# A convolution and Fourier kernel: channels c and c+16 share a Fourier block, and two intermediate layouts are turned round

## The chip, the cores and the metric

The kernel runs on one core of one Trainium2 chip. The metric is the device time of one execution in microseconds (us), the median over several runs. The program is written engine by engine: TensorE (PE; its weight loads are PEld), VectorE (DVE), ScalarE (ACT), GpSimd (POOL) and SyncE (SP, which issues transfers). Each engine runs its own list in order and waits on semaphores.

## The reference, cut to what matters

The input x is (8, 32, 64, 64): 8 images, 32 channels, 64 rows, 64 columns, all float32. A prologue (a per-pixel adaptive 3x3 filter) makes a new x. Then four layers follow, each of which is

```python
z = conv3x3(x, Kj); z = batchnorm(z); z = relu(z); z = conv3x3T(z, Kj)
x = batchnorm(x + 0.1 * z)
# per channel, with a real table t (channel x 64 x 64):
x = real(ifft2(fft2(x) * t))
```

The last line is the Fourier part. It is a sum over columns (W), a sum over rows (H), a multiplication by the table, and the way back over H and then W. The change touches the data between these sums.

## The kernel before, in words

Images are taken in four pairs (bp = 0 to 3), and each pair in four quarters (q = 0 to 3), so there are 16 steps of each kind in a layer and 64 in the four layers. A convolution step is 12 matmuls of 128x32 weights on 128x512 of data; each float32 matmul is two matmul instructions and two weight loads, so it shows as x24 in the trace. The four column tiles of a convolution (32 columns of the array each) run side by side.

The Fourier part of a quarter goes through these steps, each into one PSUM bank of 128x512, emptied by the engine named:

- `turn` (L958): four transposes put the image columns and the two images of a pair on the partitions; ACT empties them into `turned` (`keep_turned`, L491), 64 times one instruction of 128x512. Before, `turned` holds for each channel its 64 rows side by side, "(c h)": neighbouring channels of one row, which is how the bank is read, are 64 elements (256 bytes) apart.
- `fwdW` (L969): four matmuls; the stationary operand, which the weight load brings in, is the data (128 neighbouring elements of `turned`, two channels of 64 rows), and the moving operand is the constant C_FW. DVE empties the bank with four copies of 64x256 (`keep_fwdW`, L765) into `freqw`. The first quarter of a pair waits for all four `turn` quarters of it.
- `slot0`, `fwdH`, `slot0c` (L978, L985, L993): here the data moves and a constant is stationary. `slot0` waits for all four `fwdW` quarters of the pair. It moves 64 columns that stand 32 elements (128 bytes) apart; `slot0c` moves 64 columns that are neighbours. DVE multiplies by the table into `spec` (L772, L783).
- `invH` (L1003): four matmuls whose stationary operand is the data in `spec` (neighbouring elements) and whose moving operand is C_IH. The bank is emptied by four instructions of 64x256 into `backw` (`back_from_h`): by ACT (L504), or for the quarters q = 1 and 3 of pairs 2 and 3 by DVE (L789). `backw` is one of two buffers, which the profile names work (even pairs) and spare (odd pairs). Before, it holds for each image row h the 32 channels, "(h c e)": the rows of one channel, which is how the bank is read, are 32 elements (128 bytes) apart.
- `invW` (L1014): four matmuls with 128 neighbouring elements of `backw` as the stationary operand (4 image rows of 32 channels) and C_IW moving. ACT empties it into x with the batchnorm's scale (L517).

The order of steps on PE is written out by hand in `layer_steps` and is the same for all engines: the first Fourier pairs stand between the steps of the second convolution (L840 with Z), pairs 2 and 3 in a stretch without convolutions, and the last `invH` and `invW` steps between the first steps of the next layer's first convolution (L840 with X). Eight banks are handed out in that order, and a step waits until its bank's former use has been emptied.

Of the kernel before, what the change touches and what calls it, by code (L numbers as in the profile page):

```python
# [6 lines left out]
B, C, H, W = 8, 32, 64, 64  # L7
R = 128 // C
G = H // R
# [16 lines left out]
CH = 4  # L26
# [9 lines left out]
C_ID, C_FW, C_FH, C_IH, C_IW, C_HH, C_HC, C_AVG, C_ERE, C_EIM = (128 * i for i in range(10))  # L36
# [9 lines left out]
P_L = P_GB + 2  # L46
P_L9 = P_L + C * 3
P_ALL = P_L9 + C * TAPS
# [96 lines left out]
def build(nc, x_in, par, w1, b1, w2, b2, cst, sel, idb, out):  # L145
# [3 lines left out]
    with ExitStack() as ctx:  # L149
# [11 lines left out]
        turned, freqw, spec, rest, backw0 = work  # L161
# [15 lines left out]
        backw = (backw0, spare[:, 0:WORK])  # L177
# [4 lines left out]
        def cm(c, n=128, k=128):  # L182
            return cstS[0:k, c:c + n]
# [15 lines left out]
        def bank(n):  # L199
            return psum[:, n % BANKS, :]  # L200
# [78 lines left out]

        def back_from_h(n, bp, q):  # L280

            src = bank(n).rearrange("p (c t h) -> p t c h", c=4, t=2)
            dst = backw[bp % 2][:, :].rearrange("p (h c e) -> p e c h", c=C // 2, e=2)[:, :, 4 * q:4 * q + 4]
            return [(dst[64 * part:64 * part + 64, e], src[64 * e:64 * e + 64, part]) for e in range(2) for part in range(2)]

        def in_dram(t, image, r):
# [111 lines left out]
        def _(act):  # L398
# [88 lines left out]
            def keep_turned(j, c):  # L487
                n, q = NUMBER["turn", j, c], c % Q
                bk.full(n)
                dst = turned[:, :].rearrange("p (c h) -> p h c", h=H)[:, 16 * q:16 * q + 16, :]  # L490
                nc.scalar.activation(dst, bank(n).rearrange("p (h c) -> p h c", c=C),  # L491
                                     ACT.Identity).then_inc(drained[n % BANKS], 1)

            def keep_slot0(j, bp):
# [5 lines left out]
            def keep_invH(j, c):  # L500
                n = NUMBER["invH", j, c]
                bk.full(n)
                for dst, src in back_from_h(n, c // Q, c % Q):
                    last = nc.scalar.activation(dst, src, ACT.Identity)  # L504
                last.then_inc(drained[n % BANKS], 1)
# [14 lines left out]
            for j in range(DEPTH):  # L520
                for what, *at in layer_steps(j):
                    if (what, at) == ("var", [j, 1]):
                        root(j, 1)
                        act.wait_ge(bn_ready, 2 * j + 1)
                        relu_pair(j, 0)
                        for i in range(4):
                            square(j, i)
                        relu_pair(j, 1)
                        relu_pair(j, 2)
                        act.wait_ge(table_done, j + 1)  # L530
                    elif (what, at) == ("var", [j, 2]):
                        root(j, 2)
                    elif what == "turn":
                        keep_turned(*at)
                        if at == [j, Q - 1]:
                            relu_pair(j, 3)
                    elif what == "slot0c":
                        keep_slot0(*at)
                    elif what == "invH" and not turned_by_dve(at[1] // Q, at[1] % Q):
                        keep_invH(*at)  # L540
                    elif what == "invW":
                        keep_invW(*at)
                    elif what == "conv1":
                        keep_conv1(*at)
# [5 lines left out]
        def _(dve):  # L550
# [234 lines left out]
            def keep_invH(j, c):  # L785
                n = NUMBER["invH", j, c]
                bk.full(n)
                for dst, src in back_from_h(n, c // Q, c % Q):
                    last = nc.vector.tensor_copy(dst, src)  # L789
                last.then_inc(drained[n % BANKS], 1)  # L790
# [36 lines left out]
        def _(pe):  # L827
# [134 lines left out]
            def forward_w(j, c):  # L962
                n, (bp, q) = NUMBER["fwdW", j, c], divmod(c, Q)
                bk.claim(n)
                for i in range(Q if q == 0 else 0):
                    bk.result(NUMBER["turn", j, bp * Q + i])
                for i in range(4):
                    p = (4 * q + i) * 128
                    last = nc.tensor.matmul(bank(n)[:, 128 * i:128 * i + 128], turned[:, p:p + 128],  # L969
                                            cm(C_FW), start=True, stop=True)  # L970
                last.then_inc(filled[n % BANKS], 1)

# [34 lines left out]
            def inverse_w(j, c):  # L1007
                n, (bp, q) = NUMBER["invW", j, c], divmod(c, Q)
                bk.claim(n)
                for i in range(Q if q == 0 else 0):  # L1010
                    bk.result(NUMBER["invH", j, bp * Q + i])
                for g in range(CH):
                    p = (CH * q + g) * 128
                    last = nc.tensor.matmul(bank(n)[:, 128 * g:128 * g + 128], backw[bp % 2][:, p:p + 128], cm(C_IW),  # L1014
                                            start=True, stop=True)
                last.then_inc(filled[n % BANKS], 1)

            for j in range(DEPTH):
                for what, *at in layer_steps(j):
                    if what == "table":  # L1020
                        table(*at)
                    elif what == "mean":
                        average(what, *at, mean_in, 0)
                    elif what == "var":
                        average(what, *at, var_in, 4)
                    elif what == "conv1":
                        conv1(*at)
                    elif what == "conv2":
                        conv2(*at)
                    elif what == "turn":  # L1030
                        turn(*at)
                    elif what == "fwdW":
                        forward_w(*at)
                    elif what == "fwdH":
                        forward_h(*at)
                    elif what == "slot0":
                        slot_0(*at)
                    elif what == "slot0c":
                        slot_0_back(*at)
                    elif what == "invH":  # L1040
                        inverse_h(*at)
                    elif what == "invW":
                        inverse_w(*at)


def constants():

    n = np.arange(64)
    th = 2 * np.pi / 64
    k = np.arange(SL)  # L1050
    cos, sin = np.cos(th * np.outer(n, k)) / 8, np.sin(th * np.outer(n, k)) / 8
    alternating = np.cos(np.pi * n) / 8
    c = np.zeros((128, C_ALL), np.float64)
    c[:, C_ID:C_ID + 128] = np.eye(128)

    fw = np.stack([cos, -sin], 1)
    fw[:, 1, 0] = alternating
    c[:, C_FW:C_FW + 128] = np.einsum("wts,bd->wbdts", fw, np.eye(2)).reshape(128, 128)

    iw = np.stack([2 * cos, -2 * sin], 1)  # L1060
    iw[:, 0, 0], iw[:, 1, 0] = 1 / 8, alternating
    c[:, C_IW:C_IW + 128] = np.einsum("wts,bd->tbswd", iw, np.eye(2)).reshape(128, 128)


    cos, sin = np.cos(th * np.outer(n, n)) / 8, np.sin(th * np.outer(n, n)) / 8
    complex_h = np.block([[cos, -sin], [sin, cos]])
    hartley_h = np.kron(np.eye(2), cos + sin)
    c[:, C_FH:C_FH + 128] = complex_h
    c[:, C_IH:C_IH + 128] = complex_h.T
    c[:, C_HH:C_HH + 128] = hartley_h  # L1070
    c[:, C_HC:C_HC + 128] = np.round(hartley_h @ complex_h, 6)
    c[:, C_AVG:C_AVG + 128] = np.kron(np.ones((R, R)), np.eye(C)) / R
    for part in range(2):
        freq = np.where(k > 0, k, 32 * part)
        for i in range(3):
            q = part * 6 + i * 2
            a = th * n * (i - 1)
            s = slice(64 * part, 64 * part + 64)
            c[q, C_ERE:C_ERE + 128][s], c[q + 1, C_ERE:C_ERE + 128][s] = np.cos(a), -np.sin(a)
            c[q, C_EIM:C_EIM + 128][s], c[q + 1, C_EIM:C_EIM + 128][s] = np.sin(a), np.cos(a)  # L1080
            c[q, C_CS:C_CS + SL], c[q + 1, C_CS:C_CS + SL] = np.cos(th * freq), np.sin(th * freq)
            c[q, C_ONE] = 1
            c[q, C_SGN], c[q + 1, C_SGN] = 1, -1
    for form in range(2):
        c[C * form:C * (form + 3), C_MASK + form] = -1.0 / TAPS
    sel = np.zeros((3, R, TAPS, TAPS, R, C), np.float32)
    for r in range(R):
        for k in range(TAPS):
            sel[:, r, k, k, r, :] = 1
    return c.astype(np.float32), sel.reshape(3 * R * TAPS, TAPS * 128), np.eye(128, dtype=np.float32)  # L1090
# [55 lines left out]
```

## Time and profile before

| what | value |
|---|---|
| median of 3 runs | 877.1 us (876.7 to 879.67) |
| profiled execution | 876.81 us, span 875.0 us |
| mean granted TensorE clock | 0.945 of full speed |
| PE busy | 800.4 us (91%), 5704 matmul instructions |
| PEld busy | 397.6 us (45%) |
| DVE busy | 533.4 us (61%) |
| ACT busy | 396.6 us (45%) |
| prologue, up to the first Fourier step | about 240 us |
| one layer | about 173 us (the first `turn` of layers 0 and 1 starts at 240.07 and 413.61) |

A row of the trace of the form "L969 PE MATMUL psum<-cstS,work" names the line, the engine, the operation, the output and the inputs. For matmuls the moving operand stands first and the stationary one second, so "cstS,work" has the data as its stationary operand, and "work,cstS" has the data moving. "PEld LDWEIGHTS" is the load of the stationary operand; it overlaps with the matmuls before it.

### The profile page before, as it was taken

Reading aid. Unit: us, or ns where it says so; the run is one execution under the profiler, and the core shown is the slowest. Engines: PE = TensorE matmul, PEld = TensorE weight load, DVE = VectorE, ACT = ScalarE, POOL = GpSimd, SP = SyncE. Lnnn points to the kernel's source line nnn. Section 1 sums busy time; section 2 is a strip of 40 time slices with the busy share of each in tenths; the row PEclk is TensorE's granted clock in tenths of the full one; section 3 lists DMA queues with packets and bytes.
Section 4 is the critical chain, followed back from the end, with each engine's and each line's share of the span. In section 5 each row is a group of like instructions: output and inputs, shape, how many; then the busy total and the mean of one; then the engine's idle time right before and its main releaser. Section 6 shows DMA issues by size and latency. Waiting matters only on the chain.

```text
span 875.0 us, 14085 instructions
## 1 busy us (share of the span) xinstructions
PE 800.4 (91%) x5704; PEld 397.6 (45%) x5704; DVE 533.4 (61%) x982; ACT 396.6 (45%) x579; POOL 121.6 (14%) x108
## 2 busy tenths in 40 slices
PE   4698999998999799999997999899979999999793
PEld 1133333332245584432455854234568532345683
DVE  1499888964676565336765743286648332866571
ACT  1121122211855655328466643384575534736654
POOL 0277777760000000000000000000000000000000
PEclk9699899999899989998999999999989998999997
DMA  9999120209200022670000227600003274000035
GB/s 178 184 166 143 29 50 1 50 1 207 70 1 1 1 50 49 140 156 32 1 1 1 50 50 167 159 1 1 1 1 68 46 176 103 1 1 1 1 86 108
DMA packets 74570, 55.44 MB, mean 63 GB/s; under 512 B 69661, under 2 KB 69662, under 8 KB 70410
## 3 DMA queue, kind: packets, MB, share of 16 engines
q1 hardware_dynamic: 69130, 53.25, 31.6%
q10 hardware_dynamic: 5376, 1.30, 1.0%
q8 instruction: 46, 0.75, 0.4%
q14 instruction: 18, 0.15, 0.1%
HBM read 16.25 MB, written 4.19 MB: 23 GB/s over the span
## 4 chain that ended last, share of the span: by engine, by line
PE 72%; DVE 17%; SPq 3%; issue 2%; ACT 2%; DMA 1%; POOL 1%; DVEq 0%; POOLq 0%
PE psum L840 37%; DVE work L765 9%; PE psum L985 6%; PE psum L1003 5%; PE psum L1014 5%; PE psum L958 4%; PE psum L903 4%; PE psum L913 3%; SPq L296 3%; PE psum L969 2%; DVE work L789 2%; PE psum L865 2%; ACT Z L479 1%; DVE work L689 1%; POOL work L392 1%
## 5 line engine op out<-in xcount | busy, mean ns | idle before, releaser
L840 PE MATMUL psum<-Z,wts 128*32 128x512 f32 x1536 | 183.2, 621 | 2.8 <-ACT Z L479 2.5
L840 PE MATMUL psum<-X,wts 128*32 128x512 f32 x1536 | 175.2, 595 | 2.7 <-DMA X<-X 2.7
L765 DVE COPY work<-psum 64x256 f32<-64x256 f32 x256 | 107.9, 421 | 34.0 <-PE psum L969 30.3
L662 DVE BATCH_NORM_STATS2 stats<-Z 128x6 f32<-128x512 f32 x64 | 44.3, 693 | 113.1 <-ACT Z L430 113.0
L392 POOL TENSOR_TENSOR work<-work 128x512 f32<-128x512 f32 x76 | 98.9, 1301 | 74.6 <-DVE work L689 70.7
L491 ACT ACTIVATE work<-psum 128x512 f32<-128x512 f32 x64 | 63.8, 1101 | 75.2 <-PE psum L958 74.8
L430 ACT ACTIVATE Z<-psum 128x512 f32<-128x512 f32 x64 | 38.2, 596 | 129.4 <-PE psum L840 129.4
L840 PEld LDWEIGHTS psum<-Z,wts 128*32 128x32 f32 x1536 | 45.6, 113 | 112.4 <-issue 101.7
L479 ACT ACTIVATE Z<-Z,small 128x512 f32<-128x512 f32 (+1 forms) x96 | 87.6, 964 | 5.2 <-DVE small L741 4.7
L840 PEld LDWEIGHTS psum<-X,wts 128*32 128x32 f32 x1536 | 44.5, 109 | 98.7 <-issue 92.7
L756 DVE SCALAR_TENSOR_TENSOR X<-psum,X 128x512 f32<-128x512 f32 x64 | 43.8, 685 | 58.2 <-PE psum L840 56.6
L504 ACT ACTIVATE work<-psum 64x256 f32<-64x256 f32 x96 | 58.9, 614 | 30.9 <-PE psum L1003 29.8
L1003 PEld LDWEIGHTS psum<-cstS,work 128*128 128x128 f32 x512 | 58.9, 192 | 15.7 <-issue 15.7
L504 ACT ACTIVATE spare<-psum 64x256 f32<-64x256 f32 x96 | 58.6, 611 | 14.0 <-PE psum L1003 12.9
L1003 PE MATMUL psum<-cstS,work 128*128 128x128 f32 x512 | 62.8, 279 | 0.5 <-ACT work L497 0.5
L969 PE MATMUL psum<-cstS,work 128*128 128x128 f32 x512 | 63.0, 278 | 0.0
L985 PE MATMUL psum<-work,cstS 128*128 128x496 f32 x128 | 61.6, 610 | 1.3 <-DVE work L789 1.3
L969 PEld LDWEIGHTS psum<-cstS,work 128*128 128x128 f32 x512 | 59.4, 192 | 6.7 <-issue 6.7
L913 PE MATMUL psum<-work,selS 108*128 108x512 bf16 x144 | 52.6, 416 | 2.9 <-ACT work L406 1.3
L689 DVE TENSOR_TENSOR work<-Z,psum 128x512 f32<-128x512 f32 x68 | 44.4, 673 | 9.2 <-PE psum L913 8.8
L783 DVE TENSOR_TENSOR work<-psum,tabT 128x496 f32<-128x496 f32 x64 | 40.6, 666 | 11.7 <-PE psum L985 11.4
L759 DVE BATCH_NORM_STATS2 stats<-X 128x6 f32<-128x512 f32 x64 | 44.4, 694 | 2.2
(96 smaller groups left out, 796.7 us busy)
## 6 DMA issues: line engine op xcount, KB each, us to landing
X<-X SPq DMA_DIRECT2D x32, 520.0 KB, 5.4
Z<-Z SPq DMA_DIRECT2D x32, 520.0 KB, 8.5
Z<-x SPq DMA_DIRECT2D x36, 128.0 KB, 4.5
out<-Z SPq DMA_DIRECT2D x60, 64.0 KB, 1.9
X<-x SPq DMA_DIRECT2D x24, 128.0 KB, 4.5
parS<-par SPq DMA_DIRECT2D x4, 673.0 KB, 8.1
Z<-x SPq DMA_DIRECT2D x12, 120.0 KB, 4.5
X<-x SPq DMA_DIRECT2D x16, 64.0 KB, 4.9
```

What stands on the lines that cost most here:

```text
L392: nc.gpsimd.tensor_tensor(accP[c % 2], a, pool_slot[(first + k) % 4], op=ALU.add)\
L479: last = nc.scalar.activation(z, z, ACT.Relu, bias=small[p0:p1, 13:14], scale=small[p0:p1, 12:13])
L491: nc.scalar.activation(dst, bank(n).rearrange("p (h c) -> p h c", c=C), ACT.Identity).then_inc(drained[n % BANKS], 1)
L504: last = nc.scalar.activation(dst, src, ACT.Identity)
L689: nc.vector.tensor_tensor(by_line(dst), src, by_line(bank(n)), op=ALU.mult)\
L759: return nc.vector.bn_stats(stats[:, 6 * c:6 * c + 6], xc)
L765: last = nc.vector.tensor_copy(dst, src)
L840: last = nc.tensor.matmul(out_b[C * r:C * r + C, :], weights[:, o:o + C], rows(src, reg, bp, g, CH, dj - 1), start=(dj == 0), stop=(dj == ...
L913: nc.tensor.matmul(bank(n), selS[:, 128 * k:128 * k + 128], pT[0:108, N * (c % Q):N * (c % Q) + N], start=True, stop=True).then_inc(filled ...
L969: last = nc.tensor.matmul(bank(n)[:, 128 * i:128 * i + 128], turned[:, p:p + 128], cm(C_FW), start=True, stop=True)
L985: nc.tensor.matmul(bank(n)[:, 0:16 * (SL - 1)], cm(C_FH), freqw[:, N * q:N * q + N].rearrange("p (a s) -> p a s", s=SL)[:, :, 1:SL], start ...
L1003: last = nc.tensor.matmul(bank(n)[:, 128 * cp:128 * cp + 128], spec[:, p:p + 128], cm(C_IH), start=True, stop=True)
```

## The change

In `turned`, a channel pair is now (c, c+16) in place of (c, c+1), and the layout is "(e h c)": for each half of the channels and each row, 16 channels side by side. `keep_turned` reads the bank as before and writes runs of 16 neighbouring elements. `forward_w` takes its 128 stationary elements 16 elements (64 bytes) apart.

In `backw`, the layout is "(r e c g)": for each of the four row classes r and each channel, its 16 rows g side by side. The columns of C_IH are permuted so that the inverse over H brings the rows out by class, and `back_from_h` reads the bank as before and writes runs of 16. `inverse_w` takes its 128 stationary elements 16 elements apart.

The tables and constants that the host lays out follow the new channel order. `freqw`, `spec`, both moving constants' sizes, and every step's number of instructions and elements are as before.

```diff
         def back_from_h(n, bp, q):
 
-            src = bank(n).rearrange("p (c t h) -> p t c h", c=4, t=2)
-            dst = backw[bp % 2][:, :].rearrange("p (h c e) -> p e c h", c=C // 2, e=2)[:, :, 4 * q:4 * q + 4]
+            src = bank(n).rearrange("p (c t r g) -> p t c r g", c=4, t=2, r=R)
+            dst = backw[bp % 2][:, :].rearrange("p (r e c g) -> p e c r g", r=R, e=2, g=G)[:, :, 4 * q:4 * q + 4]
...
-                dst = turned[:, :].rearrange("p (c h) -> p h c", h=H)[:, 16 * q:16 * q + 16, :]
-                nc.scalar.activation(dst, bank(n).rearrange("p (h c) -> p h c", c=C),
+                dst = turned[:, :].rearrange("p (e h c) -> p h e c", e=2, h=H)[:, 16 * q:16 * q + 16]
+                nc.scalar.activation(dst, bank(n).rearrange("p (h e c) -> p h e c", e=2, c=C // 2),
                                      ACT.Identity).then_inc(drained[n % BANKS], 1)
...
                 for i in range(4):
-                    p = (4 * q + i) * 128
-                    last = nc.tensor.matmul(bank(n)[:, 128 * i:128 * i + 128], turned[:, p:p + 128],
+                    pair = turned[:, :].rearrange("p (m c) -> p c m", c=C // 2)[:, 4 * q + i]
+                    last = nc.tensor.matmul(bank(n)[:, 128 * i:128 * i + 128], pair,
                                             cm(C_FW), start=True, stop=True)
...
                 for g in range(CH):
-                    p = (CH * q + g) * 128
-                    last = nc.tensor.matmul(bank(n)[:, 128 * g:128 * g + 128], backw[bp % 2][:, p:p + 128], cm(C_IW),
-                                            start=True, stop=True)
+                    group = backw[bp % 2][:, :].rearrange("p (m g) -> p g m", g=G)[:, CH * q + g]
+                    last = nc.tensor.matmul(bank(n)[:, 128 * g:128 * g + 128], group, cm(C_IW), start=True, stop=True)
...
-    c[:, C_IH:C_IH + 128] = complex_h.T
+
+    c[:, C_IH:C_IH + 128] = complex_h.T.reshape(128, 2, G, R).transpose(0, 1, 3, 2).reshape(128, 128)
...
+    pairs = np.arange(C).reshape(2, C // 2).T.reshape(-1)
...
-                    par[j, q, P_L:P_L9] = L[j, :, 0, i, :].reshape(-1)
-                    par[j, q, P_L9:P_ALL] = L[j, :, 0].reshape(-1)
+                    par[j, q, P_L:P_L9] = L[j, pairs, 0, i, :].reshape(-1)
+                    par[j, q, P_L9:P_ALL] = L[j, pairs, 0].reshape(-1)
```

The order of instructions is the same on every engine; only the shape of some accesses on ACT and DVE differs. On DVE, where the copies of pairs 2 and 3 stand (L789: the emptying of `invH`; work and spare: its two buffers):

```order
 L765 COPY work<-psum 64x4x64 x16
-L789 COPY work<-psum 64x4x64 x8
+L789 COPY work<-psum 64x4x4x16 x8
 L772 TENSOR_TENSOR work<-psum,tabT 128x64
 L783 TENSOR_TENSOR work<-psum,tabT 128x16x31 x4
```

Nothing has moved: the eight copies stand at the same place with the same number of elements, now as runs of 16.

## Rows read from the trace of the kernel before

**Rows 1.** The page's busy times, and its chain that ended last.

```profile
PE 800.4 (91%) x5704; PEld 397.6 (45%) x5704; DVE 533.4 (61%) x982; ACT 396.6 (45%) x579; POOL 121.6 (14%) x108
PE 72%; DVE 17%; SPq 3%; issue 2%; ACT 2%; DMA 1%; POOL 1%; DVEq 0%; POOLq 0%
```

**Rows 2.** What PE waited for, 237 to 875 us: total us, times, longest.

```profile
PE psum L978 <- DVE work L765: 21.3, 8, 4.9
...
PE psum L985 <- DVE work L789: 1.3, 4, 0.3
```

**Rows 3.** Groups by line and shape, ACT and DVE: busy us, mean ns, idle before.

```profile
L491 ACT ACTIVATE work<-psum 128x512 f32<-128x512 f32 x64 | 63.8, 1101 | 75.2 <-PE psum L958 74.8
L430 ACT ACTIVATE Z<-psum 128x512 f32<-128x512 f32 x64 | 38.2, 596 | 129.4 <-PE psum L840 129.4
L504 ACT ACTIVATE work<-psum 64x256 f32<-64x256 f32 x96 | 58.9, 614 | 30.9 <-PE psum L1003 29.8
L479 ACT ACTIVATE Z<-Z,small 128x1536 f32<-128x1536 f32 x16 | 26.5, 1655 | 0.0
L479 ACT ACTIVATE Z<-Z,small 128x512 f32<-128x512 f32 x32 | 25.8, 807 | 4.9 <-DVE small L741 4.7
L765 DVE COPY work<-psum 64x256 f32<-64x256 f32 x256 | 107.9, 421 | 34.0 <-PE psum L969 30.3
L789 DVE COPY spare<-psum 64x256 f32<-64x256 f32 x32 | 19.6, 614 | 6.1 <-PE psum L1003 5.8
L566 DVE TENSOR_REDUCE ksum<-parS 128x64 f32<-128x576 f32 x4 | 4.6, 1154 | 0.0
L641 DVE TENSOR_REDUCE work<-work 128x32 f32<-128x288 f32 x8 | 3.5, 443 | 0.0
L594 DVE TENSOR_TENSOR work<-work,lsum 12x1024 f32<-12x1024 f32 x4 | 4.8, 1212 | 0.1
```

**Rows 4.** Line L978, then L993: matmuls, duration ns min/median/max.

```profile
L978 PE MATMUL psum<-work,cstS x32: 269/310/447, 257.5 to 845.6; 128*128 128x64 f32 x32
L993 PE MATMUL psum<-work,cstS x32: 219/248/275, 264.9 to 849.7; 128*128 128x64 f32 x32
```

**Rows 5.** Groups by line and shape, weight loads.

```profile
L969 PEld LDWEIGHTS psum<-cstS,work 128*128 128x128 f32 x512 | 59.4, 192 | 6.7 <-issue 6.7
L840 PEld LDWEIGHTS psum<-X,wts 128*32 128x32 f32 x1536 | 44.5, 109 | 98.7 <-issue 92.7
L1014 PEld LDWEIGHTS psum<-cstS,work 128*128 128x128 f32 x256 | 29.7, 192 | 6.8 <-issue 6.8
```

**Rows 6.** Timeline, 486 to 490 us, weight loads: start us, us, what.

```profile
486.29 3.54 PEld L1014 LDWEIGHTS psum<-cstS,work 128*128 128x128 f32 x31 [0.23 <-issue]
```

**Rows 7.** Timeline, 421 to 534 us, PE: pieces of the layer.

```profile
425.78 2.05 PE L969 MATMUL psum<-cstS,work 128*128 128x128 f32 x16
...
431.02 0.44 PE L978 MATMUL psum<-work,cstS 128*128 128x64 f32 x2 [0.48 <-DVE work L765]
...
438.60 1.04 PE L958 MATMUL psum<-cstS,X 128*128 128x128 f32 x8
...
503.19 1.93 PE L985 MATMUL psum<-work,cstS 128*128 128x496 f32 x4 [0.34 <-DVE work L789]
```

**Rows 8.** Timeline, 470 to 480 us, PE and DVE.

```profile
470.32 1.95 PE L969 MATMUL psum<-cstS,work 128*128 128x128 f32 x16
...
475.51 3.48 DVE L765 COPY work<-psum 64x256 f32<-64x256 f32 x8
479.14 0.64 PE L978 MATMUL psum<-work,cstS 128*128 128x64 f32 x2 [4.86 <-DVE work L765]
...
479.59 1.90 PE L958 MATMUL psum<-cstS,X 128*128 128x128 f32 x8
```

**Rows 9.** Stretches: PE, PEld, DVE, ACT, POOL busy; PEclk; DMA share, GB/s.

```profile
474.00:479.00 5.00, 0.28 (x3) 0.09 (x1) 4.75 (x15) 3.64 (x7) 0.00 (x0) 1.00 0.00 0
479.00:481.00 2.00, 1.86 (x9) 1.89 (x10) 0.22 (x1) 0.33 (x1) 0.00 (x0) 0.54 0.00 0
```

## The prediction

> **What bounds the kernel now.** I read the page first, then what PE waits for, then the timeline of one whole layer, and last the groups by shape. The page has PE at 91% of the span, and 72% of the chain that ended last is PE's; ACT is busy for 45% and holds 2% of the chain [rows 1]. The list of PE's waits says how little anyone holds it up from 237 us on, where the four layers stand: 21.3 us in eight waits of `slot0` for DVE's copies of `fwdW` (L765), and small change beside it. Of all of it only 1.3 us is a wait for an instruction that the change rewrites, DVE's L789, and no wait for one of ACT's two lines that it rewrites is in the list [rows 2]. So the layers are a PE-bound program with one hole of 4.86 us in each layer [rows 8] and two of 0.3 to 0.5 us [rows 7]. The reader should take from this that PE time is worth its own size almost everywhere, and ACT or DVE time is worth almost nothing.
>
> **What the change takes away.** ACT's emptying of `turn` takes 1101 ns; the same size with neighbouring writes takes 596 (L430) [rows 3]. With runs of 16 I take 596, since L765 writes runs of 32 and shows no surcharge of the kind. That is 64 x 0.505 = 32 us of ACT. The emptying of `invH` takes 614 ns on ACT. A plain element costs it (1655 - 807)/1024 = 0.83 ns (L479), so 256 plain ones would take 596 - 256 x 0.83 = 384, which for 192 instructions is 44 us of ACT. On DVE, L789 goes from 614 to about L765's 421, 0.19 us for each of 64 copies, 12 us. All of this lies beside PE's work. What reaches PE is the 0.34 us before the second `fwdH` of pair 3 [rows 7], once a layer: 1.3 us in all. I count the ACT and DVE savings at nothing beyond that; the work that hides them is PE's own, and as the change makes PE longer the cover only grows.
>
> **What it adds.** PE loads the data of `fwdW` and `invW` as the stationary operand: 512 + 512 loads of 128x128 float32 [rows 5]. No load of the trace takes its elements with a stride, so its price has to be bounded by neighbours.
>
> First the load as it is. 128 columns take 192 ns and 32 columns 109 [rows 5], 0.86 ns for each further column. In a dense stretch 31 loads take 3.54 us [rows 6]; less the length of the last one, the spacing is (3.54 - 0.19)/30 = 0.112 us. The matmul behind a load starts at the same pace: 16 in 2.05 us [rows 7], less 0.28 for the last, is 0.118. Load and matmul are about equally long, so a longer load shows at once.
>
> Then the strided accesses that the trace does have, each against a plain one:
> - ACT writing 256 bytes apart: (1101 - 596)/512 = 0.99 ns an element more; 128 bytes apart, (614 - 384)/256 = 0.90 [rows 3].
> - DVE reading 128 bytes apart (L566): 576 elements in 1154 ns. Plain reads cost (1212 - 443)/(1024 - 288) = 1.045 ns each above a fixed part (L641, L594), so a plain one would be 443 + 288 x 1.045 = 744. The surcharge is 410/576 = 0.71 ns [rows 3].
> - PE moving 64 columns 128 bytes apart: 310 ns against 248 with neighbours, 62/64 = 0.97 ns a column [rows 4].
>
> With each engine's plain pace added (0.83 ns for ACT, 1.05 for DVE) an element comes to about 1.8 ns in the first two; two engines with different paces end at one number, which speaks for a limit of the memory and not of the engine. I expect the load to end there too. Taken from the nearest row, PE's own, a load costs 128 x 0.97 = 124 ns more; by DVE's surcharge it is 91, by ACT's 127; the bound from below is nothing, if loads read by another path than moving data does.
>
> The Trainium skill bears on it twice. Its page "SBUF — State Buffer", in the box on cachelines, says that an access which goes to a new 16-byte line each time pays a penalty; by that rule a stride of 16 float32 pays for every element, and the forecast below is what it would make. Its page "TensorE: Matmul & The Clock Gate", section "LDWEIGHTS", prices a load by its columns alone, which would leave the load as it is. The first is borne out by the strided rows above, for every engine that they show; the second agrees with the two plain lengths, and no row shows it under a stride.
>
> **The sum.** A step has 8 loads: 8 x 0.124 = 0.99 us more. There are 64 `fwdW` and 64 `invW` steps: 128 x 0.99 = 127 us (91 ns gives 93, 127 ns gives 130).
>
> Off this goes what the holes take up, per layer:
> - The hole before pair 2's `slot0` [rows 8]. Its four `fwdW` steps start at 470.32. With 8 loads at 0.236, a step takes 1.89, four with the small matmul between them end near 478.1. DVE needs 1.74 a step, so it now keeps up, and only its last step follows: 478.1 + 0.15 + 1.74 + 0.14 = about 480.2 against 479.14. PE's 4.0 us more cost 1.1; 2.9 are absorbed.
> - The 0.48 before pair 0's `slot0` and the 0.34 before pair 3's `fwdH` [rows 7], 0.8 together. After the longer steps DVE is done first at both.
>
> That is 3.7 a layer, 15 in four. `slot0` of pair 3 comes after four `fwdW`, four `invH` and four `invW` steps and shows no wait in the timeline: PE was the later one, and eight steps of 0.99 come in full. So do the steps between convolutions, and the last eight `invW` steps of the last layer, behind which the stores only follow.
>
> One more term: after the hole PE runs at about half clock, 0.54 granted from 479 to 481 [rows 9], the lower of its levels of 1.2 and 2.4 GHz, after a stretch with 0.28 us of work in 5. The hole will be about 2 us. If it no longer drops the clock, some 1.5 us a layer come back (a `turn` takes 1.90 there [rows 8] and 1.04 elsewhere [rows 7], and two stand there); I take half of four times that, 3 us.
>
> 876.8 (the profiled execution; its span is 875.0) + 127 - 15 - 3 = 986. The median of the runs is 877.1, so the execution stands for it. I say 985, with its own range from 876.8 + 93 - 15 - 6 = 949 to 876.8 + 130 - 3.7 = 1003.
>
> **The rivals.**
> - *The load does not feel the stride.* For it: a load runs on its own beside the matmuls, and the price of the strided rows is known for moving data, DVE and ACT only. Against it: its plain pace, 0.86 ns a column [rows 5], is no faster than ACT's, so it has no spare pace in which to hide 1.8 ns. Then only the 1.3 us of L789 and a few tenths remain: 875, not slower. It decides as soon as the load's spacing stays under the matmul's 0.118. Chance 0.15.
> - *Part of the surcharge.* The load waits less than moving data does, say a spacing of 0.16: 1024 x 0.042 = 43, the holes take some 10, 910. For it only that the stride of 64 bytes is shorter than the 128 and 256 of the rows. Chance 0.06.
> - *The clock falls as well.* In `fwdW` and `invW` stretches the array would work half of the time, and the clock did fall after the idle hole [rows 9]. The convolution or transform behind such a stretch would then lose what the two transposes lose there, about 1.5 us, at about six places a layer: 36 us above the forecast, 1021. Against it: loads go on without a gap, and PE is never idle. Chance 0.04.
>
> **Numbers.** The forecast itself has 0.75. The range has to reach below its own 949 to hold 8 in 10: from 905 to 1010 it holds the forecast and nearly all of the partial case and leaves out the first rival and the last. Of the first rival's 0.15, I give 0.05 to faster by over 0.3% (2.6 us, about what a measurement of this kernel can tell from no change), if the quicker emptying opens more than I see, and 0.10 to within 0.3%. The rest, 0.85, is slower.
>
> **What would show it.** Right: loads of L969 and of the `invW` line at 192 + 124 = about 316 ns, eight of them 0.236 apart; `invH`'s loads (L1003) still at 192; L491 at about 600, L504 near 380 and L789 near 420; PE's wait for L765 before pair 2's `slot0` down to about 2 us; a layer of about 200 us in place of 173. The sum is wrong in size if the load's length is between 192 and 316; the reasoning is wrong if the loads stay at 192, or if they are at 316 and the span grows by far less than 109, because then matmuls did not wait for them as I think.

## The result, and the profile after

| | before | changed |
|---|---|---|
| median | 877.35 us | 966.41 us |
| profiled span | 875.0 us | 965.2 us |
| mean granted clock | 0.945 | 0.946 |

The median before is of four runs, of which the 877.1 above took three. The ratio is 1.101, with a 95% interval of 1.0988 to 1.1033: the change costs 89 us. The prediction had 985, with a range of 905 to 1010. The direction and the mechanism were right; the sum was 19 us too high.

The page of the changed kernel, its busy times and its chain (against [rows 1]):

```profile
PE 913.4 (95%) x5704; PEld 510.4 (53%) x5704; DVE 523.2 (54%) x982; ACT 326.6 (34%) x579; POOL 121.8 (13%) x108
PE 84%; DVE 6%; SPq 3%; issue 2%; ACT 1%; DMA 1%; POOL 1%; DVEq 0%; POOLq 0%
```

ACT has 70 us less to do and DVE 10 us less, and PE and its loads have 113 us more each. The chain moved the same way: DVE's 17% became 6%, and PE's 72% became 84%.

Groups by line and shape of the changed kernel (against [rows 3, 5]; columns as there):

```profile
L969 PEld LDWEIGHTS psum<-cstS,work 128*128 128x128 f32 x512 | 113.9, 311 | 6.7 <-issue 6.7
L1003 PEld LDWEIGHTS psum<-cstS,work 128*128 128x128 f32 x512 | 59.0, 192 | 15.7 <-issue 15.7
L1014 PEld LDWEIGHTS psum<-cstS,work 128*128 128x128 f32 x256 | 57.0, 311 | 6.4 <-issue 5.9
L491 ACT ACTIVATE work<-psum 128x512 f32<-128x512 f32 x64 | 35.5, 595 | 127.8 <-PE psum L958 127.8
L504 ACT ACTIVATE work<-psum 64x256 f32<-64x256 f32 x96 | 36.3, 379 | 63.4 <-PE psum L1003 62.3
L789 DVE COPY spare<-psum 64x256 f32<-64x256 f32 x32 | 13.5, 422 | 6.1 <-PE psum L1003 5.7
```

The two kinds of load that became strided went from 192 to 311 ns. The loads of `invH` (L1003), whose data still stands side by side, did not move. The emptying instructions came out as forecast: 595 against 596, 379 against 384, 422 against 421.

What PE waited for in the changed kernel, 237 to 966 us (against [rows 2]):

```profile
PE psum L978 <- DVE work L765: 9.3, 4, 2.3
PE psum L945 <- DVE small L716: 3.5, 3, 1.2
PE psum L1003 <- ACT work L497: 0.5, 1, 0.5
```

The hole before pair 2's `slot0` (the idle time of PE there) shrank from 4.86 to 2.31 us, and the two small ones are gone. The same place in the PE timeline of the changed kernel (against [rows 8]), second layer:

```profile
497.83 3.84 PE L1003 MATMUL psum<-cstS,work 128*128 128x128 f32 x32
501.50 3.65 PE L969 MATMUL psum<-cstS,work 128*128 128x128 f32 x16
...
505.13 3.74 PE L969 MATMUL psum<-cstS,work 128*128 128x128 f32 x16
511.18 0.66 PE L978 MATMUL psum<-work,cstS 128*128 128x64 f32 x2 [2.31 <-DVE work L765]
511.65 1.90 PE L958 MATMUL psum<-cstS,X 128*128 128x128 f32 x8
...
519.32 7.04 PE L1014 MATMUL psum<-cstS,work 128*128 128x128 f32 x32
526.20 0.33 PE L993 MATMUL psum<-work,cstS 128*128 128x64 f32 x2
```

Two things are to be seen. The 32 matmuls of four `invW` steps take from 519.32 to 526.20, 0.215 us each, so matmuls do wait for their loads. And the `turn` behind the hole still takes 1.90 us: 2.31 us of idling dropped the clock as 4.86 had done.

### The profile page after: what moved, and what is told of

Its sections match the earlier page's. It is cut to its first block, busy times and chain, and to the rows that moved or that the text cites. A ratio compares the mean times of both kernels' runs of the same rounds, so it can differ in the third digit from the quotient of the medians.

```text
span 965.2 us, 14085 instructions
## 1 busy us (share of the span) xinstructions
PE 913.4 (95%) x5704; PEld 510.4 (53%) x5704; DVE 523.2 (54%) x982; ACT 326.6 (34%) x579; POOL 121.8 (13%) x108
## 4 chain that ended last, share of the span: by engine, by line
PE 84%; DVE 6%; SPq 3%; issue 2%; ACT 1%; DMA 1%; POOL 1%; DVEq 0%; POOLq 0%
PE psum L840 36%; PE psum L1014 12%; PE psum L969 10%; PE psum L1003 6%; PE psum L985 6%; PE psum L958 4%; PE psum L903 3%; PE psum L913 3%; SPq L296 3%; DVE work L765 3%; PE psum L865 2%; POOL work L392 1%; ACT Z L479 1%; PE psum L978 1%; DVE work L689 1%
## 5 line engine op out<-in xcount | busy, mean ns | idle before, releaser
L765 DVE COPY work<-psum 64x256 f32<-64x256 f32 x256 | 108.1, 422 | 64.3 <-PE psum L969 60.6
L969 PE MATMUL psum<-cstS,work 128*128 128x128 f32 x512 | 117.6, 384 | 0.0
L969 PEld LDWEIGHTS psum<-cstS,work 128*128 128x128 f32 x512 | 113.9, 311 | 6.7 <-issue 6.7
L491 ACT ACTIVATE work<-psum 128x512 f32<-128x512 f32 x64 | 35.5, 595 | 127.8 <-PE psum L958 127.8
L1003 PEld LDWEIGHTS psum<-cstS,work 128*128 128x128 f32 x512 | 59.0, 192 | 15.7 <-issue 15.7
L1003 PE MATMUL psum<-cstS,work 128*128 128x128 f32 x512 | 62.8, 279 | 0.5 <-ACT work L497 0.5
L1014 PEld LDWEIGHTS psum<-cstS,work 128*128 128x128 f32 x256 | 57.0, 311 | 6.4 <-issue 5.9
L1014 PEld LDWEIGHTS psum<-cstS,spare 128*128 128x128 f32 x256 | 56.8, 311 | 5.0 <-issue 5.0
L517 ACT ACTIVATE X<-psum,small 128x512 f32<-128x512 f32 x48 | 37.4, 778 | 62.7 <-PE psum L1014 62.7
L1014 PE MATMUL psum<-cstS,spare 128*128 128x128 f32 x256 | 58.3, 384 | 0.0
L1014 PE MATMUL psum<-cstS,work 128*128 128x128 f32 x256 | 57.9, 382 | 0.0
L504 ACT ACTIVATE work<-psum 64x256 f32<-64x256 f32 x96 | 36.3, 379 | 63.4 <-PE psum L1003 62.3
```

The lines of the kernel that those rows point to most:

```text
L969: last = nc.tensor.matmul(bank(n)[:, 128 * i:128 * i + 128], pair, cm(C_FW), start=True, stop=True)
L1003: last = nc.tensor.matmul(bank(n)[:, 128 * cp:128 * cp + 128], spec[:, p:p + 128], cm(C_IH), start=True, stop=True)
L1014: last = nc.tensor.matmul(bank(n)[:, 128 * g:128 * g + 128], group, cm(C_IW), start=True, stop=True)
```

## The experiments

Ratios are to runs of the kernel before on the same chip.

**The strided loads alone.** The kernel before, with this edit:

```diff
-                    p = (4 * q + i) * 128
-                    last = nc.tensor.matmul(..., turned[:, p:p + 128], cm(C_FW), ...)
+                    pair = turned[:, :].rearrange("p (m c) -> p c m", c=C // 2)[:, 4 * q + i]
+                    last = nc.tensor.matmul(..., pair, cm(C_FW), ...)
...
+                    group = backw[bp % 2][:, :].rearrange("p (m g) -> p g m", g=G)[:, CH * q + g]
```

> The kernel before with the strided stationary operands of the change alone: fwdW and invW take their 128 elements 16 apart, the writes of the emptying instructions stay as they were (so the transforms read other elements than they should, and the output is not the reference's). Theory A (the whole loss is the load's spacing, and the quicker emptying is worth 1 to 2 us): 967 to 969 us, loads at 312 ns and 0.217 apart, L491 still 1101 and L789 still 614. Rival B (the strided load is only part of the loss, the rest comes from the new form of the writes or from what ACT and DVE now do at other times): clearly under 960 us.

Measured: 965.7 us, ratio 1.1008 (1.0986 to 1.1031), the same as the whole change's 1.101. Its loads are at 312 ns and its emptying is as slow as before (1101 ns for L491, 639 for L504, which had 614). So the loads are the whole loss, and the 80 us of ACT and DVE busy time that the change saves are worth nothing beside them. The time fell 1.3 us below what was expected, which the interval (2 us either way) allows.

**One of the two layouts.** The changed kernel with `backw`, its writes and its loads put back to rows of neighbours:

```diff
-            dst = backw[bp % 2][:, :].rearrange("p (r e c g) -> p e c r g", r=R, e=2, g=G)[:, :, 4 * q:4 * q + 4]
+            dst = backw[bp % 2][:, :].rearrange("p (h e c) -> p e c h", c=C // 2, e=2)[:, :, 4 * q:4 * q + 4]
...
+                    p = (CH * q + g) * 128
+                    last = nc.tensor.matmul(..., backw[bp % 2][:, p:p + 128], cm(C_IW), ...)
```

> The changed kernel with the half on backw undone: turned is in the new layout and fwdW loads with a stride of 16, backw is written row by row (runs of one) and invW loads neighbouring elements. Theory A: 64 steps at +0.86 us are 55 us, less the holes before slot0 of pairs 0 and 2 (0.48 and 2.55 us a layer, 12 in all): 877 + 55 - 12 = 920 us (916 to 924). Rival B (each load costs the 0.124 us of the prediction somewhere that the timeline hides): 928 or more. Rival C (the cost hangs on both layouts together, by contention between engines on the memory): not the sum; the other half would be other than 966 - 920 = 46.

Measured: 917.5 us, ratio 1.0454 (1.043 to 1.0478). PE's waits are those of the changed kernel (9.2 us in four for L765; the wait for L789 is gone too). The first half costs 40 us, and the rest of the change's 89 is 49; the half on `backw` was not run alone. They are unequal as theory A has it, which takes the holes' part off the first. That part is larger than its 12 us: from the first `turn` to the last matmul PE takes 39.4 us more than before. A strided step takes 0.853 us longer (two of them put the PE timelines 1.71 us further apart), 64 of them 54.6, so the holes took 15.2, which explains the 2.5 us under the forecast. From this kernel to the changed one the same stretch grows by 54.2 us, the plain price of 64 steps. The loads of L969 take 311 ns here as there, and those of L1014 192. So the traces show no cost that hangs on both layouts together.

**The quick emptying without the strided load.** The kernel before; the instructions walk in the order of their destination, so the stride is in the read of PSUM:

```diff
-                dst = turned[:, :].rearrange("p (c h) -> p h c", h=H)[:, 16 * q:16 * q + 16, :]
-                nc.scalar.activation(dst, bank(n).rearrange("p (h c) -> p h c", c=C),
+                dst = turned[:, :].rearrange("p (c h) -> p c h", h=H)[:, :, 16 * q:16 * q + 16]
+                nc.scalar.activation(dst, bank(n).rearrange("p (h c) -> p c h", c=C),
...
-            src = bank(n).rearrange("p (c t h) -> p t c h", c=4, t=2)
+            src = bank(n).rearrange("p (c t h) -> p t h c", c=4, t=2)
```

> The kernel before, with its layouts and loads, but the emptying instructions walk in the order of their destination: keep_turned reads PSUM 32 elements apart and writes runs of 16, back_from_h reads PSUM 128 elements apart and writes 4 elements 2 apart. Nothing is left out. Theory A (ACT and DVE time is worth nothing here; the cover of PE is complete): 875 to 878 us whatever the emptying takes, with L491 near 600 ns if a strided read of PSUM is free on ACT. Rival B (quicker emptying opens up bank waits): under 872 us. Rival C (a strided read of PSUM costs what a strided write of SBUF does): L491 stays at 1100 ns and the time at 877.

Measured: 873.97 us, ratio 0.9956 (0.994 to 0.9972). The groups by line and shape of this kernel:

```profile
L504 ACT ACTIVATE work<-psum 64x256 f32<-64x256 f32 x96 | 37.2, 388 | 42.5 <-PE psum L1003 41.5
L491 ACT ACTIVATE work<-psum 128x512 f32<-128x512 f32 x64 | 35.6, 595 | 105.3 <-PE psum L958 105.1
L1014 PEld LDWEIGHTS psum<-cstS,work 128*128 128x128 f32 x256 | 29.7, 192 | 6.8 <-issue 6.8
```

ACT reads PSUM 32 or 128 elements apart at its plain pace. So everything that the change wanted from ACT and DVE can be had without touching the loads, and it is worth 3.9 us (2.5 to 5.3 by the interval), between theory A's 875 and rival B's 872. Two places of the trace account for it. The wait for L789 before pair 3's second `fwdH` is gone, and with it that place becomes 0.60 us shorter a layer, 2.4 in all. The other lies at the end, where ACT's slow emptying held up its own L517, whose results the output stores wait for. First the kernel before, then this one:

```profile
851.63 4.99 ACT L504 ACTIVATE spare<-psum 64x256 f32<-64x256 f32 x8 [1.31 <-PE psum L1003]
856.65 5.61 ACT L517 ACTIVATE Z<-psum,small 128x512 f32<-128x512 f32 x8
...
850.68 1.59 ACT L504 ACTIVATE spare<-psum 64x256 f32<-64x256 f32 x4 [1.31 <-PE psum L1003]
852.46 1.57 ACT L504 ACTIVATE spare<-psum 64x256 f32<-64x256 f32 x4 [0.20 <-PE psum L1003]
854.25 7.03 ACT L517 ACTIVATE Z<-psum,small 128x512 f32<-128x512 f32 x8 [0.21 <-PE psum L1014]
```

SP can begin its last 28 stores at 856.0 in place of 858.2, while PE is only 1 us ahead of the kernel before, and from the last matmul to the end of the span it is 11.8 us in place of 13.6. No list of PE's waits shows this part. Single executions are a blunt measure for it: one layer of the kernel before can differ from another by 2.4 us of the same run (the starts of pair 2's `slot0` stand 173.55, 171.16 and 173.56 apart), with PE's granted clock at its lower level for about 17 us of the first and the third of these and for about 10 us of the second.

**A ladder of strides.** Each quarter loads with its own stride, on a line of its own:

```diff
-                    pair = turned[:, :].rearrange("p (m c) -> p c m", c=C // 2)[:, 4 * q + i]
...
+                    if q == 0:
+                        last = nc.tensor.matmul(o, turned[:, i:i + 127 * 2 + 1:2], cm(C_FW), start=True, stop=True)
+                    elif q == 1:
+                        last = nc.tensor.matmul(o, turned[:, i:i + 127 * 3 + 1:3], cm(C_FW), start=True, stop=True)
```

> The changed kernel with another stride in each quarter, one line each: fwdW loads with strides of 2, 3, 4 and 8 elements for q = 0 to 3, invW with 15, 5, 1 and 12 (so the transforms take other elements than they should, and the output is not the reference's). Theory A (the cost comes when each element falls in another 16-byte line): strides 1, 2 and 3 load in 192 ns (3 perhaps a little above), strides 4, 5, 8, 12, 15 all in 312. Rival B (cost grows with the distance, or comes from powers of two, as banks would make it): 5 and 15 near 192, or 4 and 8 below 312. Rival C (any stride but 1 pays): 2 and 3 at 312.

Measured: 947.6 us in a single run. The timeline of its weight loads, 8 loads to a step (L970 to L976: strides 2, 3, 4, 8; L1021 to L1027: 15, 5, 1, 12):

```profile
335.94 1.92 PEld L1021 LDWEIGHTS psum<-cstS,spare 128*128 128x128 f32 x8
337.76 1.86 PEld L1023 LDWEIGHTS psum<-cstS,spare 128*128 128x128 f32 x8
339.53 0.99 PEld L1025 LDWEIGHTS psum<-cstS,spare 128*128 128x128 f32 x8
340.44 2.21 PEld L1027 LDWEIGHTS psum<-cstS,spare 128*128 128x128 f32 x8
...
326.25 1.03 PEld L970 LDWEIGHTS psum<-cstS,work 128*128 128x128 f32 x8
327.19 1.48 PEld L972 LDWEIGHTS psum<-cstS,work 128*128 128x128 f32 x8
328.59 1.95 PEld L974 LDWEIGHTS psum<-cstS,work 128*128 128x128 f32 x8
330.45 2.00 PEld L976 LDWEIGHTS psum<-cstS,work 128*128 128x128 f32 x8
```

With the median length of one load from the view of each line, and the spacing as (eight loads less one length)/7:

| stride, elements | 1 | 2 | 3 | 4 | 5 | 8 | 12 | 15 | 16 (changed kernel) |
|---|---|---|---|---|---|---|---|---|---|
| length, ns | 192 | 197 | 262 | 329 | 316 | 334 | 369 | 326 | 312 |
| spacing, us | 0.114 | 0.119 | 0.174 | 0.231 | 0.221 | 0.238 | 0.263 | 0.228 | 0.217 |

Two elements apart is all but free, three costs half of the surcharge, and from four on (16 bytes) the loads follow each other at about twice the spacing, whatever the distance. That is theory A's threshold, with a middle at 3 that it had only half expected. Rival B's banks fall as the cause: 5 and 15 are as slow as 4 and 8. Something of that kind lies on top, though: from 4 on, theory A had one length, and the measured ones run from 312 to 369, with 12 the slowest and the 16 of the change the quickest. What sets this stays open. The page "SBUF — State Buffer" of the Trainium skill, in its box on cachelines, has full pace as long as two accesses hit a 16-byte line; that fits 1, 2 and the step at 4. It fits 3 as well: three apart, of every four elements two share a line and two stand alone, which makes half of the surcharge, and the load gained 70 ns where four apart gained 137. The page "TensorE: Matmul & The Clock Gate" of the Trainium skill, section "LDWEIGHTS", prices a load by its columns, which holds only for the first two places of the table.

**Filling the hole, kernel before.** The four `invH` steps of pair 1 are moved behind `fwdW` of pair 2:

```diff
-    steps += quarters("invH", j, 1) + quarters("fwdW", j, 2, first) + [("mean", j, 2)] + quarters("fwdW", j, 2, second)
+    steps += quarters("fwdW", j, 2, first) + [("mean", j, 2)] + quarters("fwdW", j, 2, second) + quarters("invH", j, 1)
```

> The kernel before with one move in the order of steps: the four invH steps of pair 1 stand behind the four fwdW steps of pair 2 in place of ahead of them, so PE has 3.7 us of work while DVE empties those fwdW steps. Theory A (the hole before pair 2's slot0 is DVE's lag, and any PE work put there is free): the wait of 4.86 us goes to about 1.1, the clock no longer drops behind it, 5 us a layer: 857 to 862 us. Rival B (ACT's slow emptying of invH, 614 ns x 16, now ends later and holds the banks or the turn steps): a new PE wait for L504 or L491, gain under 8 us: 868 or more.

Measured: 871.5 us, ratio 0.9929 (0.9914 to 0.9944). Rival B. What PE waited for in this kernel:

```profile
PE psum L985 <- ACT spare L504: 8.8, 8, 1.4
PE psum L978 <- DVE work L765: 8.3, 8, 1.6
PE psum L945 <- DVE small L716: 4.8, 7, 1.2
```

The hole went from 4.87 to 1.62, and 2.2 us a layer of waiting for ACT's emptying of `invH` came in its place. Here ACT's time has a price on PE's own path. The other half of theory A failed too: the clock still drops in all four layers, now behind three shorter waits that stand close together. The second layer's, with one stretch in the columns of [rows 9]:

```profile
474.18 0.44 PE L978 MATMUL psum<-work,cstS 128*128 128x64 f32 x2 [1.62 <-DVE work L765]
477.37 1.10 PE L985 MATMUL psum<-work,cstS 128*128 128x496 f32 x2 [0.83 <-ACT spare L504]
479.83 4.33 PE L985 MATMUL psum<-work,cstS 128*128 128x496 f32 x6 [1.36 <-ACT spare L504]
...
480.00:482.00 2.00, 2.00 (x3) 0.99 (x4) 0.21 (x2) 2.00 (x4) 0.00 (x0) 0.50 0.00 0
```

**The same move in the changed kernel.**

> The changed kernel with the same move. Its hole is 2.31 us. Theory A: the hole and the half clock behind it go, 2.3 + 1.5 us a layer, 15 in all: 951 us (948 to 955). If the move gives the same here as in the kernel before, the hole did not absorb any of the change's extra PE time; theory A says that it absorbed 2.5 us a layer, so the move must be worth about 10 us less here.

Measured: 946.4 us, ratio 1.0787 (1.0768 to 1.0805), 20 us under the changed kernel and 1.6 under the range expected. From the first of the moved steps to the first `invW` of pair 0 the two kernels' PE timelines have 21.8, 21.5, 20.5 and 21.7 us in the four layers against 17.3 in all four: 16 us of the 20, near the 15 of theory A. Of the rest, 2.5 us are the later start of the layers in the changed kernel's profiled execution (243.40 against 240.87). The 2.31 us hole is gone, a wait of 0.48 for L504 has come, and the clock does not fall there. The comparison in the second half of the expectation missed: the move alone brings the kernel before less, not more, because there the slow ACT takes it back.

**The move with the quick emptying.** Both edits above in the kernel before.

> The kernel before with the move and with the emptying in the order of the destination (L491 595 ns, L504 388, L789 423). If ACT's time has become worth something after the move (rival B above), this is faster than the move alone by more than the 4 us that the quicker emptying gave without it; if not, by those 1 to 4 us: 853 to 858.

Measured: 856.3 us, ratio 0.9754 (0.9737 to 0.9771). PE's waits for ACT's L504 are gone, and in the PE timeline the same place reads:

```profile
466.08 2.03 PE L969 MATMUL psum<-cstS,work 128*128 128x128 f32 x16
467.95 3.74 PE L1003 MATMUL psum<-cstS,work 128*128 128x128 f32 x32
473.30 0.44 PE L978 MATMUL psum<-work,cstS 128*128 128x64 f32 x2 [1.62 <-DVE work L765]
473.57 1.05 PE L958 MATMUL psum<-cstS,X 128*128 128x128 f32 x8
```

The hole of 1.62 us, now without the two waits for L504 behind it, no longer drops the clock: the `turn` behind it takes 1.05 and not 1.90, and the granted clock stays at full speed. The stretch from `fwdW` to `invW` is 15.4 us in every layer, against 19.6 to 21.1 before. The quicker emptying, worth 4 us by itself, is worth 15 on top of the move (871.5 to 856.3), so ACT's time has become worth something, the first of the two cases expected. Repeated beside the last run below:

> The move and the emptying in the order of the destination once more, as the neighbour of the run with the stores shared: 856 us, 0.975 of the kernel before.

it took 853.8 us, ratio 0.973 (0.9714 to 0.9745). Its three full layers take 167.2 us each in both traces; the first `turn` starts at 243.24 in one and at 239.44 in the other, so two runs of one kernel can lie 3.8 us apart by their prologues.

**The stores at the end.** 16 of SP's 60 output stores go to GpSimd, which walks through the last layer's `invW` results of pairs 1 and 2:

```diff
-                        if (bp, h, image) != (BP - 1, 1, 1):
+                        if (bp, h, image) != (BP - 1, 1, 1) and not (image == 1 and bp in (1, 2)):
                             store(sp, bp, image, G // 2 * h, G // 2 * h + G // 2)
```

> The kernel before with 16 of the 60 output stores of SP issued by GpSimd, which is idle there (second images of pairs 1 and 2); nothing else. Theory A (the last 12.6 us are SP working off its queue of stores at 0.55 to 0.65 us each, so the changed kernel's last 6.8 us of longer invW steps were hidden by that queue): SP is done about 8 us earlier, the end moves to about 5 to 6 us behind the last emptying, as in the changed kernel: 5 to 7 us faster, 871 us. Rival B (the end is set by the transfers themselves or by the DMA engines, not by their issue): no change within 1 us. Rival C (GpSimd's issue is slow and ends last): slower.

Measured: 874.7 us, ratio 0.9966 (0.9955 to 0.9977), 3 us where theory A had 5 to 7. From the last matmul to the end it is 10.9 us in place of 13.6. With 20 stores moved, on top of the best kernel:

> The best so far (the move of the four invH steps and the emptying in the order of the destination) with the output stores shared better than in the first try: GpSimd issues the second image of pairs 1 to 3 but for the last half pair, 20 stores, and SP 40. Theory A (what is left behind the last emptying is SP's queue of stores): about 5 us under the run beside it without that edit. Rival B (the stores' own transfers set the end): within 1.5 us of it.

Measured: 852.9 us, ratio 0.971 (0.9691 to 0.973), 0.9 us under its neighbour, whose interval it overlaps. By the medians this is rival B's figure. The traces say a little more: from the last matmul to the end it is 9.3 us against the neighbour's 11.7, and 1.3 us of that gain are hidden by a later start of the layers (240.70 against 239.44). So the truth lies between the two theories. Its stretch around the last matmuls (PE, PEld, DVE, ACT, POOL busy, clock, DMA share, GB/s) says why:

```profile
840.00:845.00 5.00, 0.58 (x6) 0.39 (x4) 0.00 (x0) 1.28 (x2) 3.50 (x7) 0.98 0.97 184
```

With the issue shared between three queues the DMA engines are busy for 97%, against 72% in the kernel before from 865 to 870 us, and SP's last stores follow each other 0.76 us apart in place of 0.53. There is a backlog of stores, and SP's issuing is only one part of what works it off slowly; the transfers are the next limit right behind.

## Why the prediction was right, and where its sum was off

The ledger below sets the prediction's terms against the two PE timelines, in which the steps stand in the same order and can be subtracted one by one.

| term | predicted | measured |
|---|---|---|
| 128 steps with longer loads | +127 | 128 x 0.853 = +109.2 |
| holes that absorb it | -15 | -14.8 |
| the clock no longer falls | -3 | it still falls; -0.8 left over |
| the end of the last layer | 0 | -6.8 |
| the prologue | 0 | +3.3 |
| sum | +109 | +90.1 |

The load's term makes 18 of the 19 us. The other misses come to about nothing together (-7 at the end, +2 at the clock, +3 in the prologue), which is luck.

*What bounds the kernel.* Right, and shown: the loads alone make the whole difference. The quicker emptying alone makes 4 us, where the prediction had 1.3: pair 3's place gives 0.6 us a layer in place of 0.34, and the 1.8 us at the queue of stores were counted "at nothing beyond that".

*The price of a strided load.* The mechanism was right and the size was off. The term was 128 x 0.97 ns = 0.124 us a load, from the moving data's row; it measured 0.119 in length (311 - 192) but only 0.103 to 0.107 in spacing (0.217 or 0.215 against 0.112; 0.853 a step by eight). The step of the prediction that put this too high is "a load costs 128 x 0.97 = 124 ns more", used for the spacing. A load is longer than its spacing (80 ns with neighbours, 95 with the stride), and what the length gained was more than the pace lost. The DVE row (91) and PE's row (124) bracketed it. The ladder shows that a stride of 16 was also the cheapest of those from 4 up; a stride of 12 would have cost 0.15.

*The holes.* Right within 1 us in the sum, by two small misses that cancel: pair 2's hole gave 2.6 us a layer (4.87 became 2.31) in place of 2.9, and pair 3's place 0.6 in place of 0.34. Pair 0's went as worked out.

*The clock.* The prediction gave it half a chance to stay up, for a hole of about 2 us. It fell. A stretch of the changed kernel, columns as in [rows 9]:

```profile
511.00:513.00 2.00, 1.82 (x9) 1.85 (x10) 0.26 (x2) 0.27 (x1) 0.00 (x0) 0.50 0.00 0
```

0.50 is the lower level, 1.2 of 2.4 GHz, behind 2.31 us without a matmul. Behind the 1.62 us of the moved order it stayed up when nothing followed, and fell when waits of 0.83 and 1.36 us followed, so no single length of a hole decides it. The prediction looked at 2 us behind the hole; the clock stays low for 3.2 to 7.0 us there in the kernel before and for 3.4 to 7.0 in the changed one. The move of the steps in the changed kernel prices this at a little over 2 us a layer (21.4 - 17.3, less the hole's 2.31, and with the new wait of 0.48 added), where the prediction had 1.5. There is a second such place in both kernels: between two layers, where PE has matmuls of 12 rows (L938) and of one column (L945) and a wait of 1.17 us, the clock is low for 6.7 to 10.3 us. The rival in which the long strided stretches bring the clock down is refuted: in the changed kernel the clock is at 1.00 from 519 to 544 us, through `invW`, `fwdW` and `invH`, and low at the same seven places as before.

*The end.* "the last eight `invW` steps of the last layer, behind which the stores only follow" was wrong. From the start of those steps to the end of the span it is 20.9 us before and after, though the steps take 6.8 us more. The SP queue's rows of the timeline in a window from the end of the last matmul on (each counts one store that was already being issued), first the kernel before, from 861.44 us:

```profile
861.05 12.11 SPq L300 DMA_DIRECT2D out<-Z  x22
```

and the changed kernel, from 958.38:

```profile
958.30 5.01 SPq L300 DMA_DIRECT2D out<-Z  x9
```

SP issues its last 28 stores without a break, 0.5 us apart, from the time when the first two of the eight steps are emptied: from 858.2 to 872.7 before, from 948.8 to 962.8 after. The eight steps take 7.3 us before and 14.1 after; the stores, begun some 4 us into them, take 14 us either way and outlast both. So 21 of 60 stores were still to be issued when the last `invW` matmul ended, and 8 after; the longer steps fell into that backlog. The run with `turned` alone agrees: its `invW` is quick, and from the last matmul to the end it has 13.6 us, as the kernel before, against 6.8 in the changed one. The page had SP's queue at 3% of the chain that ended last, and the prediction did not ask what that was. The two store experiments confirm a backlog (2.6 and 2.5 us less behind the last matmul) but not that SP's issuing alone sets it.

*The prologue.* The first `turn` starts at 240.07 before and at 243.40 after. It starts between 239.4 and 243.2 in the ten other traces, all with the same prologue, and 3.8 us apart in two runs of one kernel, so I take this for scatter and not for the change.

## What to carry to other kernels

When data is the stationary operand of small matmuls, its layout belongs to the weight load, since load and matmul ran at one pace here (0.112 and 0.118 us) and any surcharge showed in full. Put a stride where it costs nothing, which here was ACT's and DVE's read of PSUM, and only then look at writes and loads of SBUF. Busy time saved on an engine that hardly anybody waits for is worth little until the order is changed so that someone does: the same emptying was worth 4 us alone and 15 behind the move. And look at what follows the last matmul: there the longer steps cost nothing, and ACT's quicker emptying gained 1.8 us that no wait of PE shows.

## What the runs showed of the hardware

- A 128x128 float32 weight load takes 192 ns with neighbouring elements, 197 two apart, 262 three apart, and 312 to 369 from four apart on.
- ACT's and DVE's reads of PSUM 128 and 512 bytes apart carry no surcharge: 595 ns for 128x512 against 596 with neighbours, 388 and 423 for 64x256 against 379 and 422 in the changed kernel, whose reads are of neighbours.
- Writes of runs of 16 float32 go at the plain pace (595 ns), and so do those two elements apart (388 ns on ACT).
- The TensorE clock fell to 0.50 behind an idle hole of 2.31 us in all four layers, and in all four behind waits of 1.62, 0.83 and 1.36 us that stand close together. It stayed at full speed behind the 1.62 us alone.
- A backlog of output stores leaves SP 0.53 to 0.55 us apart with the DMA engines at a share of 0.72; with three queues issuing, the share is 0.97 and SP's stores are 0.66 to 0.76 apart.
